# Scores that choose context rows, in a perceiver kernel: each full-precision product becomes three one-pass products of split parts

## Reference

```
qp = einsum('bld,ed->ble', q, Wq)              # q: normalized x, 2 x 128 x 512
scores = einsum('bld,bmd->blm', qp, kv)        # kv: the context, 2 x 2048 x 512
idx = argmax(scores, axis=-1)                  # one context row for each token
mem = take_along_axis(kv, idx[..., None], axis=1)
mkv = einsum('bld,ed->ble', mem, Wkv)          # 32 key and 32 value columns
logits = einsum('bhld,bmd->bhlm', qh, mk) * scale     # 16 heads, 128 x 128
out = einsum('bhlm,bmd->bhld', softmax(logits), mv); return out @ Wc.T
```

## Time and profile before

| | us |
|---|---|
| median of 3 runs | 1375.26 |
| lowest, highest | 1368.37, 1378.55 |
| the profiled execution, its time | 1376.37 |
| its span, first to last instruction | 1374.5 |
| PE busy | 1304.3 (95%) |
| DVE busy | 917.4 (67%) |
| ACT busy | 700.5 (51%) |

### The profile page before, as it was taken

How to read it: one execution, slowest core, us unless ns; L and a number is a source line. 1 busy time by engine, 2 the same in 40 slices (tenths; PEclk the granted TensorE clock), 3 DMA queues, 4 the chain that set the end, 5 groups by cost and what they waited for, 6 DMA issues and landing times.

```text
span 1374.5 us, 22698 instructions
## 1 busy us (share of the span) xinstructions
PE 1304.3 (95%) x9348; PEld 1095.9 (80%) x9348; DVE 917.4 (67%) x1219; ACT 700.5 (51%) x870; POOL 16.5 (1%) x19
## 2 busy tenths in 40 slices
PE   7999999999999999885899999999888999999998
PEld 6899899979999997665677888888655679888886
DVE  4566565666666666688779999999715577555553
ACT  4534444444444444471367777777503444666552
POOL 0000000000000000000000000000010010000000
PEclk9999999999999999986899999999989999999999
DMA  8101011401010011201058999999950044555552
GB/s 289 36 24 44 21 36 40 132 27 36 28 36 20 20 63 62 92 34 61 32 210 330 351 361 345 352 346 347 356 215 16 31 158 181 183 191 196 186 188 77
DMA packets 50219, 197.65 MB, mean 144 GB/s; under 512 B 12112, under 2 KB 20560, under 8 KB 30416
## 3 DMA queue, kind: packets, MB, share of 16 engines
q1 hardware_dynamic: 47792, 187.41, 37.5%
q0 software_dynamic: 2336, 8.91, 1.8%
HBM read 195.78 MB, written 0.52 MB: 143 GB/s over the span
## 4 chain that ended last, share of the span: by engine, by line
PE 84%; DVE 10%; ACT 2%; issue 2%; DMA 2%; SPq 0%; DVEq 0%; ACTq 0%
PE psum L454 13%; PE psum L429 13%; PE psum L2274 9%; PE psum L1547 7%; PE psum L481 5%; PE psum L2275 4%; PE psum L506 4%; PE psum L1570 4%; PE psum L1550 4%; PE psum L2257 3%; PE psum L1573 2%; PE psum L2288 2%; PE psum L1864 2%; PE psum L465 1%; PE psum L1584 1%
## 5 line engine op out<-in xcount | busy, mean ns | idle before, releaser
L1613 DVE TENSOR_TENSOR arena_r<-ring,arena_r 128x2048 fp32r<-128x2048 f32 x96 | 219.6, 2289 | 31.1 <-ACT arena_r L1607 30.9
L454 PE MATMUL psum<-ring_r,arena_r 128*128 128x256 f32 x1536 | 200.8, 289 | 2.6 <-ACT arena_r L724 2.5
L429 PE MATMUL psum<-arena_r 128*128 128x512 f32 x768 | 185.6, 397 | 9.8 <-ACT arena_r L758 9.5
L454 PEld LDWEIGHTS psum<-ring_r,arena_r 128*128 128x128 f32 x1536 | 191.3, 193 | 3.3 <-issue 2.7
L1607 ACT CAST arena_r<-ring 128x2048 fp32r<-128x2048 f32 x96 | 183.4, 1914 | 16.5 <-PE psum L1550 9.5
L2274 PE MATMUL psum<-arena_r 128*128 128x512 f32 x512 | 179.2, 396 | 1.1 <-DVE arena_r L2337 1.1
L429 PEld LDWEIGHTS psum<-arena_r 128*128 128x128 f32 x768 | 143.0, 190 | 42.0 <-issue 8.8
L2275 PE MATMUL psum<-arena_r 128*128 128x256 f32 x512 | 142.8, 279 | 0.0
L2228 DVE TENSOR_TENSOR arena_r<-ring,arena_r 128x2048 fp32r<-128x2048 f32 x43 | 98.6, 2292 | 62.0 <-ACT arena_r L2223 62.0
L1547 PE MATMUL psum<-arena_r 128*128 128x512 f32 x512 | 129.5, 395 | 1.3 <-issue 1.3
L2274 PEld LDWEIGHTS psum<-arena_r 128*128 128x128 f32 x512 | 96.1, 188 | 24.3 <-DVE arena_r L2337 1.2
(11 more groups left out here) (320 smaller groups left out, 1851.7 us busy)
## 6 DMA issues: line engine op xcount, KB each, us to landing
ring<-in_stream SPq DMA_DIRECT2D x151, 1024.0 KB, 4.8
arena<-in_ctxT POOLq DMA_DIRECT2D x8, 1024.0 KB, 12.5
arena<-in_ctxT SPq DMA_DIRECT2D x7, 1024.0 KB, 8.6
arena<-in_wk SPq DMA_DIRECT2D x16, 256.0 KB, 3.2
wv_in<-in_wv SPq DMA_DIRECT2D x8, 512.0 KB, 3.3
arena<-in_wq SPq DMA_DIRECT2D x16, 256.0 KB, 2.6
arena<-in_wk SPq DMA_DIRECT2D x16, 128.0 KB, 3.1
arena<-in_wo SPq DMA_DIRECT2D x2, 1024.0 KB, 6.1
```

What stands on the lines that cost most here:

```text
L429: last = nc.tensor.matmul(bank, wk_sb[wp][:, c, w], cx[xp][kb][:, c, :], start=c == wp == xp == 0, stop=c == C - 1 and xp == 1)
L454: last = nc.tensor.matmul(bank[:, q * T:(q + 1) * T], cx[xp][kc // 4][:, c, kc % 4 * P:(kc % 4 + 1) * P], wv_sb[wp][:, c, :], start=c == w ...
L1613: nc.vector.tensor_tensor(mwlo[p % MB], ring[(BLK_MOE + p) % RING][:, :], mwhi[p % MB].bitcast(fp32), ALU.subtract).then_inc(moe_lo if p < ...
```

## The change

The scores are made as split products. `cx1[0]` (four hi blocks, shared by the batches) and `cx1[1][b][kb]` (lo, written over the fp32 context in place) are views of the arena; `qp_parts` holds hi and lo of qp. ScalarE makes the hi blocks and the hi halves of qp, and afterwards the fp32 `qpT`, which `logits` still use. VectorE makes the lo blocks and halves. The hi blocks of batch 1 wait for the scores of the same block of batch 0 (`pick_scores`), whose hi block they overwrite. `ctx_back` becomes three semaphores: blocks 0 and 1, blocks 2 and 3, and batch 1. On VectorE the maximum over three blocks is separated (`first_max_dve`), and `pick_dve(1)` comes ahead of `spread_mk(0)`. TensorE does all blocks of batch 1 but the last lo product ahead of the turn of batch 0's rows; 8 `keep_clock` calls come ahead of `logits(0)`, and the 7 behind them, with the wait for the index, go.

```
@@ -1806,6 +1806,10 @@
         la = view(20480, B, H, P)
         laT = view(24576, B, H, P)
         x1oT = view(28672, C, T)
+        cx1 = [[view(20480 + kb * C * 512, C, 512, one_pass=True) for kb in range(KB)],
+               [[view((b * KB + kb) * C * 512, C, 512, one_pass=True) for kb in range(KB)] for b in range(B)]]
+        qp_parts = [view(29696 + i * C * T, C, T, one_pass=True) for i in range(2)]
         mvt = sb("mvt", [P, B, DK])
         top8 = [sb(f"top8_{b}", [P, 8]) for b in range(B)]
         top16 = [sb(f"top16_{b}", [P, 16]) for b in range(B)]
@@ -1815,10 +1819,13 @@
         nlm = sb("nlm", [P, B, H])
         ls = sb("ls", [P, B, H])
-        ctx_back = [sem(f"ctx_back{b}") for b in range(B)]
+        ctx_back = [sem(f"ctx_back{i}") for i in range(3)]
         x1_proj = sem("x1_proj")
         qp_ready = sem("qp_ready")
         pick_scores = sem("pick_scores")
         top_found = sem("top_found")
         at_found = sem("at_found")
@@ -1844,6 +1851,7 @@
         PICK_BANK = (4, 0)
         MEM_BANK, MK_BANK, MV_BANK = (4, 0), (6, 1), (7, 2)
         X1_BANK = (5, 6)
+        CTX_SPLITS = ctx_count(B - 1, KB - 1, 0)
         LA_SCALE = float(1.0 / np.sqrt(DK).astype(np.float32))
         def cross1_pe(pe):
@@ -1858,12 +1866,21 @@
                     last.then_inc(x1_proj if ec == 1 else blk_used, 1)
             pe.wait_ge(qp_ready, 2)
-            def pick_part(b, parts):
-                for n in parts:
-                    kb, c = n // C, n % C
-                    last = nc.tensor.matmul(psum[:, PICK_BANK[b] + kb, :], qpT[:, c, b * P:(b + 1) * P],
-                                            ctxT_sb[b][kb][:, c, :], start=c == 0, stop=c == C - 1)
-                return last
+            def pick_hi(b, kb):
+                pe.wait_ge(ctx_hi, CTX_SPLITS + b * KB + kb + 1)
+                for i in range(2):
+                    if b == kb == 0 and i == 1:
+                        pe.wait_ge(q_ready, NU + 2)
+                    for c in range(C):
+                        nc.tensor.matmul(psum[:, PICK_BANK[b] + kb, :], qp_parts[i][:, c, b * P:(b + 1) * P],
+                                         cx1[0][kb][:, c, :], start=c == i == 0, stop=False)
+            def pick_lo(b, kb):
+                pe.wait_ge(ctx_lo, CTX_SPLITS + b * KB + kb + 1)
+                for c in range(C):
+                    last = nc.tensor.matmul(psum[:, PICK_BANK[b] + kb, :], qp_parts[0][:, c, b * P:(b + 1) * P],
+                                            cx1[1][b][kb][:, c, :], start=False, stop=c == C - 1)
+                last.then_inc(pick_scores, 1)
             def turn_mem(b):
                 pe.wait_ge(mem_arrived[b], 16)
@@ -1905,19 +1922,20 @@
                 return nc.tensor.matmul(psum[:, X1_BANK[b], :], x1oT[:, c, b * P:(b + 1) * P], block(BLK_X1 + 1)[:, c, :],
                                         start=c == 0, stop=c == C - 1)
-            pe.wait_ge(ctx_back[0], KB * 16)
-            pick_part(0, range(0, 12)).then_inc(pick_scores, 1)
-            pick_part(0, range(12, 16)).then_inc(pick_scores, 1)
-            pe.wait_ge(ctx_back[1], KB * 16)
-            pick_part(1, range(0, 8))
+            for kb in range(KB):
+                pick_hi(0, kb)
+                pick_lo(0, kb)
+            pe.wait_ge(qp_ready, 4)
+            for kb in range(KB - 1):
+                pick_hi(1, kb)
+                pick_lo(1, kb)
+            pick_hi(1, KB - 1)
             turn_mem(0)
-            pick_part(1, range(8, 10))
+            pick_lo(1, KB - 1)
             project_mem(0)
-            pick_part(1, range(10, 12)).then_inc(pick_scores, 1)
-            pick_part(1, range(12, 16)).then_inc(pick_scores, 1)
+            keep_clock(pe, 5, 8)
             logits(0)
-            pe.wait_ge(at_found, 2)
-            keep_clock(pe, 3, 7)
             turn_mem(1)
             project_mem(1)
             logits(1)
@@ -1946,12 +1964,31 @@
         def cross1_act(act):
             norm_act(act, 3)
+            def split_hi(b, kb):
+                if b == 0:
+                    act.wait_ge(ctx_back[kb // 2], 2 * 16)
+                else:
+                    act.wait_ge(ctx_back[2], KB * 16)
+                    act.wait_ge(pick_scores, kb + 1)
+                nc.scalar.copy(cx1[0][kb], ctxT_sb[b][kb]).then_inc(ctx_hi, 1)
+            def copy_qp(out, i):
+                nc.scalar.copy(out[:, 2 * i:2 * i + 2, :], psum[:, 2 + i, :].rearrange("p (c t) -> p c t", c=2)).then_inc(qp_ready, 1)
+            split_hi(0, 0)
+            split_hi(0, 1)
+            act.wait_ge(x1_proj, 1)
+            copy_qp(qp_parts[0], 0)
+            split_hi(0, 2)
+            act.wait_ge(blk_used, BLK_X1 + 1)
+            copy_qp(qp_parts[0], 1)
+            split_hi(0, 3)
             for i in range(2):
-                if i == 0:
-                    act.wait_ge(x1_proj, 1)
-                else:
-                    act.wait_ge(blk_used, BLK_X1 + 1)
-                nc.scalar.copy(qpT[:, 2 * i:2 * i + 2, :], psum[:, 2 + i, :].rearrange("p (c t) -> p c t", c=2)).then_inc(qp_ready, 1)
+                act.wait_ge(q_ready, NU + i + 1)
+                copy_qp(qpT, i)
+            for kb in range(KB):
+                split_hi(1, kb)
             def copy_mem(b):
                 act.wait_ge(memT_filled, b + 1)
@@ -1999,11 +2036,25 @@
         def cross1_dve(dve):
             norm_dve(dve, 3)
+            def split_lo(b, kb):
+                dve.wait_ge(ctx_hi, CTX_SPLITS + b * KB + kb + 1)
+                lo_part(cx1[1][b][kb], ctxT_sb[b][kb], cx1[0][kb]).then_inc(ctx_lo, 1)
+            def split_qp(i):
+                dve.wait_ge(qp_ready, i + 1)
+                lo_part(qp_parts[1][:, 2 * i:2 * i + 2, :], psum[:, 2 + i, :].rearrange("p (c t) -> p c t", c=2),
+                        qp_parts[0][:, 2 * i:2 * i + 2, :]).then_inc(q_ready, 1)
+            def scores_of(b):
+                return psum[:, PICK_BANK[b]:PICK_BANK[b] + 4, :].rearrange("p a n -> p (a n)")
+            def first_max_dve(b):
+                dve.wait_ge(pick_scores, KB * b + KB - 1)
+                nc.vector.max(top16[b][:, 0:8], scores_of(b)[:, 0:1536])
             def pick_dve(b):
-                scores = psum[:, PICK_BANK[b]:PICK_BANK[b] + 4, :].rearrange("p a n -> p (a n)")
-                dve.wait_ge(pick_scores, 2 * b + 1)
-                nc.vector.max(top16[b][:, 0:8], scores[:, 0:1536])
-                dve.wait_ge(pick_scores, 2 * b + 2)
+                scores = scores_of(b)
+                dve.wait_ge(pick_scores, KB * b + KB)
                 link(dve, nc.vector.max(top16[b][:, 8:16], scores[:, 1536:]))
                 nc.vector.max(top8[b][:, :], top16[b][:, :]).then_inc(top_found, 1)
                 dve.wait_ge(top_found, b + 1)
@@ -2032,9 +2083,21 @@
                 dve.wait_ge(laT_filled, C * b + j + 1)
                 nc.vector.tensor_copy(laT[:, b, 4 * j:4 * j + 4, :], bank4(PICK_BANK[b] + j)).then_inc(laT_ready, 1)
+            split_lo(0, 0)
+            split_lo(0, 1)
+            split_qp(0)
+            split_qp(1)
+            split_lo(0, 2)
+            split_lo(0, 3)
+            split_lo(1, 0)
+            split_lo(1, 1)
+            first_max_dve(0)
+            split_lo(1, 2)
             pick_dve(0)
+            split_lo(1, 3)
+            first_max_dve(1)
+            pick_dve(1)
             spread_mk(0)
-            pick_dve(1)
             for j in range(C):
                 largest_la(0, j)
             scale_la(0, 0)
@@ -2453,7 +2516,7 @@
                         gp.wait_ge(blk_used, BLK_X1 - 8 + 4 * kb)
                     elif b == 0 and kb == 2:
                         gp.wait_ge(moe_added, 1)
-                    gp.dma_start(ctxT_sb[b][kb], ctxT[b][:, :, kb * 512:(kb + 1) * 512]).then_inc(ctx_back[b], 16)
+                    gp.dma_start(ctxT_sb[b][kb], ctxT[b][:, :, kb * 512:(kb + 1) * 512]).then_inc(ctx_back[2 if b else kb // 2], 16)
             for b in range(B):
                 gp.wait_ge(picked, b + 1)
                 gp.indirect_dma_start(out=mem[:, b, :], out_offset=None, in_=ctx_rows,
```

## The result

Twenty runs of each kernel were timed in turn: 1374.05 us before, 1370.25 after (medians), a ratio of 0.9971 with a 95% interval of 0.9959 to 0.9982. By the ratio that is 4.0 us won (2.5 to 5.6), far inside 1%. The forecast was 5.6, to 1369.7.

The account below looks back on a forecast made before the run. PE time and two pick-to-gather latencies were taken as what can be won. The copy of batch 1's rows moves from 1055.19 to 1049.6, so 1375.26 - 5.6 = 1369.7 us; own range 1367 to 1373, with scatter 1362.5 to 1376.5.

Parts of the forecast that it names:

- The products: Scores on TensorE: 64 records of 0.429 us become 96 of 0.229, 27.5 to 22.0, winning 5.5 us.
- Rival D: Scores: split operands come late each time, so TensorE follows VectorE; gain 2 to 3 us, 1373; chance 0.05.
- Rival C: Behind the stage: the gain is given back to weights or another late wait; 1375.3; chance 0.06.
- Batch 0's pick: VectorE: the 2.7 us TensorE wins on batch 0 are spent there; the address comes at the same 1033.7.
- The gather: Batch 0's rows: issued at 1033.96, taken as 3.98 us beside a subtraction, against 3.34 before; TensorE idles 0.75.
- Rival A: Batch 0's gather waits until VectorE's two-SBUF-operand subtraction ends, rows 2.0 us later; gain 3.6, 1371.6; chance 0.12.
- Logits, exponentials, the copy: Path to the end: logits(0) at 1044.65, first exponential 2.06 later, eight exponentials 2.9; copy of batch 1's rows at 1049.6.
- Behind the copy: After the copy of batch 1's rows: same instructions in the same order, so the 5.6 us gain stays.
- Rival B: Turn of batch 0's rows: a late gather idles TensorE 3.7 us and the clock halves; slower, 1378.2; chance 0.04.
- The sum: Whole kernel: 5.6 us off the median of 1375.26 gives 1369.7, own range 1367 to 1373.

Follow-up runs that it names:

- Pick first: Changed kernel with batch 0's pick ahead of the subtraction of batch 1's block 2 on VectorE; ratio to the kernel before 0.9958 (0.9940 to 0.9976).
- maxima beside: Changed kernel, two one-SBUF-operand maxima and an 8-column subtraction replacing batch 1 block 3's subtraction, its lo part left out; first product to last addition 56.39 us.
- old order behind: Changed kernel's split products with the old order of fillers, key spreading and index wait behind the scores; ratio to the kernel before 0.9982 (0.9955 to 1.0009).
- no subtraction beside: Changed kernel with VectorE's subtraction for batch 1's block 3 cut from 2048 to 8 columns, its lo part left out; first product to last addition 57.56 us.

## Why the prediction was right, and where it was off

**The products: right.** 0.227 a record after, 0.229 forecast; TensorE at the turn at 21.01 from the first product when nothing holds it (21.05 forecast). Rival D, that splitting doesn't speed the products, is out: TensorE ran 18.00 of 18 us. Rival C, that the gain is given back behind the stage, is out too: 295.8 us behind the last addition in both profiles.

**Batch 0's pick: right.** What TensorE wins on batch 0 goes into VectorE's queue; the gather is issued at 17.64 against 17.81 before and forecast. Pick first shows the queue as the cause: 15.44. One detail was off: batch 1's first cast waited 0.5 us for the last transfer of the context, since in this execution the stage began 1.8 us earlier and the transfers were issued 0.8 us later. In maxima beside the cast waited 1.3 us for them, and the gather was issued at 18.03.

**The gather: this is the term that was mis-sized.** I took 3.98 us, from the second gather before; it took 5.06. I had put the 3.98 down to a busy VectorE, and that was wrong as well: in old order behind the same reductions run beside the second gather, and it landed in 3.4. Rival A named the mechanism and got a chance of 0.12; no subtraction beside and maxima beside show it. Rival A's size was off too: it put a whole gather of 3.98 behind the end of the subtraction, 2.0 us more. In fact the gather waits for the rest of the subtraction that is under way, 1.9 us at that point, and takes 1.72 longer than 3.34 to land; since 0.64 were in the sum, the turn was 0.95 later than forecast, and the copy of batch 1's rows 0.7. The evidence that I held against the rival, a DMA issue of 0.94 us beside a subtraction, was from a GpSimd instruction that had begun first, and another kind of one.

**Logits, exponentials, the copy: right.** From the turn to the logits 6.67 after (6.7 forecast), from there to the copy 4.74 (4.95). ScalarE's exponentials did become what the copy waits for.

**Behind the copy: partly wrong.** "Behind the copy the same instructions follow in the same order, so 5.6 stays" took a full clock for granted. It holds in one profile of three, where the stage gained 62.59 - 57.75 = 4.8, which is 5.6 less 0.7 for the gather (to 0.1); the other two lost 0.8 and 1.1 more to half clock. Rival B had the clock fall at the turn, after a long wait; it did not, with 1.59 us of idle time there. Why it falls later, in some executions only, stays open.

**The sum.** The three stage gains, 4.1, 3.7 and 4.8, lie in the measured interval of 2.5 to 5.6; the forecast of 5.6 is at its upper edge, and too high by the 0.7 of the gather and, in two profiles of three, by the clock. Rival A's 3.6 is nearer to the 4.0, but by luck: its gather cost too much, and the clock, which it left full, made up for that. There is one profile of the kernel before to compare with, so how often its own clock falls here isn't known.

## What to carry to other kernels

Before moving work onto an engine that looks idle, list what it runs beside: here 5.5 us of cheaper products filled VectorE as well, gave back the whole gain of batch 0 to its queue, and slowed a gather that another engine issues. Put the instruction that starts a long latency (pick, then gather) ahead of the work that merely has to be done in time, and keep VectorE instructions with two SBUF operands away from GpSimd's indirect DMA (here the gather's instruction took 2.81 us beside one, and 1.02 without). When a stage gains a few us of 1375, read it from its own first instruction: the way into it differed by 2.5 us between profiles.

## What the runs showed of the hardware

- GpSimd's gather instruction takes 1.0 us alone, beside maxima with one SBUF operand or beside a key spread that reads PSUM, 2.81 beside a 2.28 us subtraction with two, 1.72 beside two of 1.2 us; it ended 0.9 us after the end of the subtraction under way both times.
- With two subtractions of 2.28 us in a row the instruction still took 2.81, but the rows landed in 6.11 us in place of 5.06; the cause of that is not shown.
- Behind 21 us in which TensorE was busy 17.9 the granted clock fell to half for some 3 us; in another execution of the same program, behind 17.7, it stayed full.
- TensorE idle for 2.48 us ahead of the logits went with half clock for some 3 us right behind it; 1.59 us idle at the turn did not.
